# A state-space scan whose outputs are read in groups of eight steps instead of four, with a ring of sixteen states

## What is computed

```python
def step(s, t):
    x_t, b_t, c_t = t
    s = jnp.clip(s * A + b_t[:, None, :] * x_t[:, :, None], -10.0, 10.0)
    y = jnp.sum(c_t[:, None, :] * s, axis=-1)
    return (s, y)
_, ys = jax.lax.scan(step, s0, xs)
```

## Time and profile before

| what | value |
|---|---|
| time, median of 3 runs | 2550.72 us (2540.39 to 2566.41) |
| the profiled execution, its own time | 2556.13 us |
| its span | 2554.1 us |
| mean granted TensorE clock in it | 0.875 |
| PE busy | 2253.7 us (88%) |
| DVE busy | 1995.5 us (78%) |
| POOL busy | 809.9 us (32%) |
| ACT busy | 725.6 us (28%) |

### The profile page before, as it was taken

How to read it: one execution, slowest core, us unless ns; L and a number is a source line. 1 busy time by engine, 2 the same in 40 slices (tenths; PEclk the granted TensorE clock), 3 DMA queues, 4 the chain that set the end, 5 groups by cost and what they waited for, 6 DMA issues and landing times. The chain is left out here.

```text
span 2554.1 us, 57186 instructions
## 1 busy us (share of the span) xinstructions
PE 2253.7 (88%) x16096; PEld 1916.9 (75%) x16096; DVE 1995.5 (78%) x6529; ACT 725.6 (28%) x1656; POOL 809.9 (32%) x1042
## 2 busy tenths in 40 slices
PE   7845877999999898989899898989898999989997
PEld 3422666888878787878788787878787887878887
DVE  3549856879797978889897989888888978798632
ACT  3430202223231423233232313132222323142323
POOL 0032203334231424333332424242333323142524
PEclk9855767989898988989898989989898989899988
DMA  7531000001010100010010101010000001010000
GB/s 268 176 107 24 23 10 18 11 11 27 8 26 10 27 10 23 11 25 12 13 25 7 27 11 27 11 27 11 23 11 18 20 11 24 9 27 6 6 1 9
DMA packets 101002, 73.43 MB, mean 29 GB/s; under 512 B 64376, under 2 KB 94592, under 8 KB 99712
## 3 DMA queue, kind: packets, MB, share of 16 engines
q1 hardware_dynamic: 100736, 70.08, 10.0%
HBM read 46.43 MB, written 23.59 MB: 27 GB/s over the span
## 5 line engine op out<-in xcount | busy, mean ns | idle before, releaser
L1394 DVE TENSOR_TENSOR decayed_state<-state,decay 128x128 f32<-128x128 f32 x2048 | 702.3, 383 | 1.0
L792 POOL TENSOR_TENSOR hs_parts<-hs_whole,hs_parts 128x256 fp32r<-128x256 f32 x640 | 488.0, 776 | 484.5 <-ACT hs_whole L916 464.6
L1404 DVE CUSTOM_DVE_ANT_0 state<-decayed_state,bank 128x128 f32<-128x128 f32 x2048 | 505.6, 285 | 34.0 <-PE bank L1006 16.2
L916 ACT ACTIVATE hs_parts<-bank,f_b_sb 128x256 fp32r<-128x256 f32 x512 | 244.8, 478 | 772.7 <-PE bank L1088 772.7
L1006 PE MATMUL bank<-xrows,brows 128*128 128x256 f32 x1024 | 261.0, 345 | 122.2 <-DVE state L1404 100.7
L1088 PE MATMUL bank<-f_w_hi,hs_parts 128*128 128x256 f32 x2048 | 348.0, 293 | 10.7 <-DVE x L1491 9.9
L1088 PEld LDWEIGHTS bank<-f_w_hi,hs_parts 128*128 128x128 f32 x2048 | 284.1, 193 | 52.7 <-ACT hs_parts L916 46.6
L1006 PEld LDWEIGHTS bank<-xrows,brows 128*128 128x128 f32 x1024 | 178.3, 216 | 178.8 <-DVE state L1404 92.2
L816 POOL TENSOR_TENSOR kv<-kv,kvm 128x272 f32<-128x272 f32 x64 | 48.8, 765 | 672.1 <-DVE kvm L1603 671.5
L916 ACT ACTIVATE hs_whole<-bank,f_b_sb 128x256 f32<-128x256 f32 x512 | 245.5, 480 | 0.0
L1088 PE MATMUL bank<-late_fT_parts,f_w_hi 128*128 128x256 f32 x1024 | 187.9, 317 | 0.5 <-DVE kvm L1603 0.5
(11 more groups left out here) (154 smaller groups left out, 3540.8 us busy)
## 6 DMA issues: line engine op xcount, KB each, us to landing
xrows<-xs_dram SPq DMA_DIRECT2D x512, 32.0 KB
brows<-bs_dram SPq DMA_DIRECT2D x1024, 2.0 KB
xt<-in_x SPq DMA_DIRECT2D x4, 1024.0 KB, 7.7
xn_dram<-xn SPq DMA_DIRECT2D x4, 1024.0 KB, 5.4
z_dram<-zT SPq DMA_DIRECT2D x4, 1024.0 KB, 4.1
f_w_sb<-in_f_w SPq DMA_DIRECT2D x2, 2048.0 KB
xs_dram<-xhi SPq DMA_DIRECT2D x4, 1024.0 KB, 4.5
xs_dram<-xlo SPq DMA_DIRECT2D x4, 1024.0 KB, 8.2
```

Of the source, the lines that this page charges most:

```text
L792: return pool.tensor_tensor(lo, whole, hi.bitcast(f32), ALU.subtract)
L916: act.activation(slot[:, m], HB[e % 2][:, m * TOK:(m + 1) * TOK], ACT.Relu, bias=g["f_b1"][:, e, m:m + 1]).then_inc(done.sem, 1)
L1394: dve.tensor_tensor(decayed_state[:, part], state[:, (s - 1) % RING, part], decay[:, part], ALU.mult).then_inc(decayed.sem, 1)
L1404: dve._custom_dve(add_sat, out=state[:, s % RING, part], in0=decayed_state[:, part], in1=U[n % 2][:, s % 2 * D + h * HALF:s % 2 * D + (h + ...
```

## The change

Outputs are made for eight steps at a time ("octet"): eight matmuls in the order of the steps, so that the column tiles are visited 0, 1, 2, 3, 0, 1, 2, 3. Each matmul has the operands, the column tile and the PSUM region that it had. The octets stand at every fourth pair, the last at the end of the pass; the first of a chunk stands at pair 4 instead of pair 2. A ring of 16 states holds eight states while the next eight are made; VectorE's waits on `y_made` are recounted for it. The ring takes 16 KB of SBUF per partition instead of 8 KB.

```diff
-RING = 8
+RING = 16
-QUADS = CT // 4
+YSTEPS = 8
+OCTS = CT // YSTEPS
+OPAIRS = YSTEPS // 2
...
-        y_made = signal("y_made", QUADS)
+        y_made = signal("y_made", OCTS)
...
-            def scan_output(i, quad):
-
-                if quad == 0:
+            def scan_output(i, oct_):
+
+                if oct_ == 0:
 
                     pe.wait_ge(y_copied.sem, y_copied.after(i, 0))
-                if quad % 2 == 0:
-                    pe.wait_ge(cblk_set.sem, cblk_set.after(i, quad // 2 + 1))
-                pe.wait_ge(stepped.sem, stepped.after(i, 8 * (quad + 1)))
-                tile, m = divmod(quad, QUADS // TILES)
-                for j in range(4):
-                    s = 4 * quad + j
+                pe.wait_ge(cblk_set.sem, cblk_set.after(i, YSTEPS // QT * (oct_ + 1)))
+                pe.wait_ge(stepped.sem, stepped.after(i, 2 * YSTEPS * (oct_ + 1)))
+                for s in range(YSTEPS * oct_, YSTEPS * (oct_ + 1)):
+                    j = s % 4
+                    tile, m = divmod(s // 4, CT // 4 // TILES)
...
-                        if n >= 2 and n % 2 == 0:
-                            scan_output(i, n // 2 - 1)
+                        if n >= OPAIRS and n % OPAIRS == 0:
+                            scan_output(i, n // OPAIRS - 1)
...
-                        if not (isinstance(i, int) and i == 0 and n < 4):
-
-                            dve.wait_ge(y_made.sem, y_made.after(i, (n - 4) // 2 + 1))
+                        if not (isinstance(i, int) and i == 0 and n < RING // 2):
+
+                            dve.wait_ge(y_made.sem, y_made.after(i, (n - RING // 2) // OPAIRS + 1))
...
-                        dve.wait_ge(y_made.sem, y_made.after(i, 2 * u))
+                        dve.wait_ge(y_made.sem, y_made.after(i, QT // YSTEPS * u))
```

More of the change, by code:

```diff
@@ L940, in step @@
                 if c is not None:
-                    act.wait_ge(y_made.sem, y_made.after(c, QUADS))
+                    act.wait_ge(y_made.sem, y_made.after(c, OCTS))
                     act.activation(turn[:].rearrange("p i d -> p (i d)"), Y[:], ACT.Copy).then_inc(y_copied.sem, 1)
@@ L1008, in scan_inputs @@
                 last.then_inc(u_made.sem, 1)
-            def scan_output(i, quad):
-                if quad == 0:
+            def scan_output(i, oct_):
+                if oct_ == 0:
                     pe.wait_ge(y_copied.sem, y_copied.after(i, 0))
-                if quad % 2 == 0:
-                    pe.wait_ge(cblk_set.sem, cblk_set.after(i, quad // 2 + 1))
-                pe.wait_ge(stepped.sem, stepped.after(i, 8 * (quad + 1)))
-                tile, m = divmod(quad, QUADS // TILES)
-                for j in range(4):
-                    s = 4 * quad + j
+                pe.wait_ge(cblk_set.sem, cblk_set.after(i, YSTEPS // QT * (oct_ + 1)))
[3 more added lines that the diff above has]
+                    tile, m = divmod(s // 4, CT // 4 // TILES)
                     slot = s % (PARTS * QT)
                     last = pe.matmul(Y[YCOLS * j:YCOLS * (j + 1), tile * D:(tile + 1) * D], cblk[:, slot * YCOLS:(slot + 1) * YCOLS],
-                                     state[:, s % RING, :], start=(m == 0), stop=(m == QUADS // TILES - 1),
+                                     state[:, s % RING, :], start=(m == 0), stop=(m == CT // 4 // TILES - 1),
                                      tile_position=(0, YCOLS * j))
@@ L1239, in step @@
                     scan(PAIRS - at_pair[0])
-                    scan_output(i, QUADS - 1)
+                    scan_output(i, OCTS - 1)
                     return
```

## The result

The changed kernel takes 2606.1 us (median of 4 runs, 2605.5 to 2614.5) where the kernel before took 2546.9 beside it: 1.0227 times as long, with a 95% interval of 1.0166 to 1.0288. It is slower by 2.3%; forecast was 0.7% faster (2533 against the 2550.7 shown). The profiled execution of the changed kernel spans 2611.2 us.

The account below looks back on a forecast made before the run. TensorE and VectorE were taken to bound the kernel in turns, so only TensorE's stretches A, C and E count. Terms of -13 and -4.5 us gave 2538.6 from 2556.1, or 2533 for the median; range 2502 to 2565.

Parts of the forecast that it names:

- The sum over single instructions: TensorE's savings and costs in the stretches it bounds: -0.88 us a pass, times 15, -13 us.
- The price of an octet: TensorE time of eight output steps in place: 1.21 us against 1.54 for two quads, saving 0.33.
- Rival 2: The second four steps do not join the first: an octet costs 1.54 us, total 2562; chance 0.12.
- A: TensorE-bound stretch from the router's result to VectorE's wait for an expert's product: +0.44 us a pass.
- C: TensorE-bound stretch among the expert products, 1030.33 to 1044.73: one octet for two quads, -0.33 us a pass.
- E: TensorE-bound stretch through attention, 1058.26 to 1111.02: three octets for six quads, -0.99 us a pass.
- The router's wait: TensorE's wait for VectorE at the router result: to grow from 2.87 us to over 3.5.
- The clock: TensorE's granted clock in attention: a small gain from the octet among the second numerators, 0.3 us a pass, -4.5 us.
- Rival 4: Fewer, larger lots hold the clock less in attention: 0.02 lower a pass, +23 us, 2574; chance 0.13.
- rival 3: The octet inside the second numerators holds the clock longer: 0.02 gained a pass, 36 us in all, 2502; chance 0.18.
- New waits: Waits added by octets and the longer ring: none seen, nothing added to the sum.
- The marks: Signs to check: passes averaging over 142 us mean rival 4; mean loop clock moving over 0.01 means the forecast is wrong.

Follow-up runs that it names:

- e8: The kernel before, with the two scan-input matmuls of pair 27 issued three times over: 2516.4 us, ratio 0.9919 to the kernel before.
- e1: The kernel before with a ring of 16 states and VectorE's wait recounted for it, quads as before: 2566.7 us, ratio 1.0094 to the kernel before.
- e13: The kernel before with a ring of 16 states in use, allocated behind all other tiles, quads as before: 2578.6 us, ratio 1.0139 to the kernel before.
- e12: The kernel before with room for 16 states set aside but only 8 used, so tiles behind lie 8 KB further: 2541.5 us, ratio 1.0022.

## Why the prediction was wrong

The sum over single instructions was right in the stretches where the clock stayed up. It was beaten by the term beside it, of which the prediction itself said that it is as large as everything else.

**The price of an octet: right.** Timeline of TensorE in the changed kernel around the octet of pair 12:

```profile
1037.86 0.40 PE L1008 MATMUL bank<-xrows,brows 128*128 128x256 f32 x2
1038.18 1.07 PE L1023 MATMUL bank<-state,cblk 128*32 128x256 f32 x16
1039.18 0.73 PE L1089 MATMUL bank<-f_w_hi,hs_parts 128*128 128x256 f32 x4
1039.75 0.64 PE L1089 MATMUL bank<-f_w_lo,hs_parts 128*128 128x256 f32 x4
```

From the scan inputs to the second four matmuls of the product is 1.89 us (forecast 1.92; 1.48 with a quad), and the 16 records span 1.07 us (forecast 1.08). Steps five to eight join the first four. Rival 2 is out. The rule that it came from ("TensorE: Matmul & The Clock Gate", Part 3, The mechanism, in the Trainium skill), that loads overlap running matmuls only in another row group, does not hold here: the second load of each column tile, in the same rows, hid under running matmuls (all 16 loads of the octet above lie in the first 0.59 us of its 1.07). The same section also lets a load be pulled ahead into a background weight buffer, and whether that is what happened no run tells.

**The stretches: A and C right, E wrong.** These are the rows that answer to the earlier trace rows, from the pass at 992.0:

```profile
1013.97 0.38 PE L1066 MATMUL bank<-ident_sb,comb 128*8 128x128 f32 x2 [3.43 <-DVE comb L1465]
...
1024.74 0.88 DVE L1492 SCALAR_TENSOR_TENSOR res<-bank,comb,res 128x256 f32<-128x256 f32 x2 [2.23 <-PE bank L1089]
...
1034.47 0.50 PE L1008 MATMUL bank<-xrows,brows 128*128 128x256 f32 x2 [0.98 <-DVE state L1405]
...
1048.38 0.88 DVE L1492 SCALAR_TENSOR_TENSOR res<-bank,comb,res 128x256 f32<-128x256 f32 x2 [0.45 <-PE bank L1089]
...
1061.72 0.51 PE L1008 MATMUL bank<-xrows,brows 128*128 128x256 f32 x2 [0.88 <-DVE state L1405]
...
1119.80 0.69 DVE L1612 TENSOR_TENSOR a_t<-bank,a_t 128x512 f32<-128x512 f32 x1 [2.83 <-PE bank L1337]
```

A went from 10.34 to 10.77 us: +0.43, forecast +0.44 (with 6.8 us at half clock in both). C went from 14.40 to 13.91: -0.49, forecast -0.33. The router's wait rose from 2.87 to 3.43, forecast over 3.5. E went from 52.76 to 58.08 us, +5.32 where -0.99 was forecast. With 29.8 us at half clock in it (10.2, and 19.6 up to 1119.80) against 17.0, the clock is worth 12.8 x 0.43 = 5.5 of the 6.3 between.

**The clock: the step that failed, in sign and in size.** The prediction took a gain of 0.3 us a pass, because the octet puts two more rounds of full columns among the second numerators. The trace of what stands there:

```profile
1101.99 3.43 PE L1313 MATMUL bank<-vv,ss 128*128 128x17 f32 x16
1105.26 0.77 PE L1008 MATMUL bank<-xrows,brows 128*128 128x256 f32 x2
1105.96 1.94 PE L1023 MATMUL bank<-state,cblk 128*32 128x256 f32 x16
1107.83 3.60 PE L1313 MATMUL bank<-vv,ss 128*128 128x17 f32 x16
1111.36 2.89 PE L1322 MATMUL bank<-vv,hs_whole 64*128 64x68 f32 x16
...
1115.98 3.78 PE L1337 MATMUL bank<-wo_sb,turn 128*128 128x256 f32 x8 [0.26 <-ACT turn L908]
```

In the kernel before two quads stand in this stretch, at 1093.66 (pair 26) and at 1099.23 (pair 28), and its clock fell behind the second, at 1100.05:

```profile
1093.66 0.64 PE L1022 MATMUL bank<-state,cblk 128*32 128x256 f32 x8
...
1095.87 0.98 PE L1304 MATMUL bank<-kv,qT 128*64 128x68 f32 x16
...
1097.12 1.85 PE L1312 MATMUL bank<-vv,ss 128*128 128x17 f32 x16
...
1099.23 0.64 PE L1022 MATMUL bank<-state,cblk 128*32 128x256 f32 x8
1099.80 3.40 PE L1312 MATMUL bank<-vv,ss 128*128 128x17 f32 x16
```

Counted from the start of its pass, that is 111.3 us, and the clock was back at 121.5. In the changed kernel it fell at 108.1 and came back at 128.6. It had fallen at 1100.2, before the octet, among the running sums and with pair 26's quad gone; the octet itself runs at half clock, 1.94 us instead of 1.07, and so does all behind it up to 1120.7. The numerators take 3.60 us; 16 of them at full clock, in e8, take:

```profile
1077.98 1.96 PE L1312 MATMUL bank<-vv,ss 128*128 128x17 f32 x16
```

So the term of the sum that failed is the clock's, -0.3 us a pass, where the runs showed +4.4. The prediction looked at what the octet brings to its place and not at what leaves the place before. Rival 4 had the mechanism in words (fewer, larger lots; the clock falls sooner and returns later), but priced it at 0.02 of clock and +36 us; it was 0.03 and the passes grew by 64 us. Its chance was put at 0.13, below rival 3's 0.18 for a gain. Its size was to be had from the earlier trace rows: if the window at 1100 doubles, 10 us more at half clock is 0.43 x 10 = 4.4 us a pass.

**New waits: none, but the ring was not free.** As forecast, the additions of VectorE wait no more than before: its waits for scan inputs are 4.1 us in all from 400 to 2400 us, against 6.4. "I see none" was still wrong as a price: 16 slots and the recounted wait cost about 1% with quads (e1, e13) without showing as a wait at their own place, a second term that the sum had at nothing. What did grow is VectorE's wait for numerators, against the earlier trace rows from 2.4 us a time to 3.7, where it was to shrink; in waits from 400 to 2400 us:

```profile
DVE rec L1595 <- PE bank L1313: 100.5, 27, 6.2
...
DVE state L1405 <- PE bank L1008: 4.1, 4, 2.9
```

**The marks.** The prediction said that passes over 142 us mean rival 4, and that it is wrong if the mean clock in the loop moves by more than 0.01. Passes took 144.8 and the clock moved by 0.03. Both marks pointed the right way. The range ended at 2565, with rival 4 at 2574 left outside it, and the kernel took 2606.

## What to carry to other kernels

When TensorE's clock moves between its two levels inside a pass, ask of each edit first what full-size work it takes away from a stretch of small matmuls, and price the half-clock window that may double there (here 0.43 us for each us), before adding up saved overheads. Gathering small lots into large ones saves their entry cost exactly as the trace says and can lose several times that by the gaps it leaves (here some 1.2 us a pass saved, 4.4 lost). And a longer ring with a looser wait is an edit to be timed by itself, even where no row shows a wait.

## What the runs showed of the hardware

- TensorE's clock fell to half while the engine was busy without a gap (10.20 of the 10.20 us before 1100.20, and 20.24 of the 20.50 behind it), in a stretch of matmuls with 17 or 68 columns or 32 rows.
- Work that is thrown away can make a kernel faster: four matmuls more a pass took half-clock time from 24.4 to 15.1 us on the kernel before (ratio 0.9919, and 0.9864 by the medians) and from 34.6 to 25.8 on the changed one (-1.7 points). Twenty did not do better than four.
- Eight matmuls over four column tiles, two for each (16 records), span 1.07 us at full clock and 1.94 at half.
- Other tiles 8 KB further on cost 0.2%, with 0 inside the interval (e12), and the use of twice as many slots 0.9 to 1.4% in kernels with quads. The cause of the latter stays open.
